# Rotary tables in two steps with a buffer of their own, squares in the projections' banks, rotation in two steps, expert scatters later

## What is computed

```python
xn = layernorm(x)
# attention: 16 query heads, 4 key/value heads, D = 128, an output gate
q, gate, k, v = split(xn @ w_qkv.T)
q = rope(layernorm(q, q_norm_w, q_norm_b))      # per head, with weight and bias
k = rope(layernorm(k, k_norm_w, k_norm_b))
attn = softmax(causal(q @ k.T / sqrt(D))) @ v
a = (attn * sigmoid(gate)) @ w_o.T
# experts: 8, the two best of each token
top, idx = top_k(xn @ w_router, 2); p = softmax(top)
f = sum_j p_j * (relu(xn @ w_fc[idx_j])**2 @ w_proj[idx_j])
return x + a + f
```

## Time and profile before

| what | value |
|---|---|
| runs, median (lowest to highest) | 1565.15 us (1564.32 to 1567.33), 3 runs |
| the profiled execution, its own time | 1559.9 us |
| its span | 1558.1 us |
| granted TensorE clock, mean | 0.998 of 2.4 GHz |

### The profile page before, as it was taken

How to read it: one execution, slowest core, us unless ns; L and a number is a source line. 1 busy time by engine, 2 the same in 40 slices (tenths; PEclk the granted TensorE clock), 3 DMA queues, 4 the chain that set the end, 5 groups by cost and what they waited for, 6 DMA issues and landing times.

```text
span 1558.1 us, 29980 instructions
## 1 busy us (share of the span) xinstructions
PE 1508.6 (97%) x10589; PEld 1379.8 (89%) x10589; DVE 1323.2 (85%) x3139; ACT 1154.4 (74%) x3013; POOL 522.8 (34%) x726
## 2 busy tenths in 40 slices
PE   4999999999899999999999999999999999999998
PEld 3788999999899999999888898999988888999997
DVE  7999888787899888787789988887778989988875
ACT  3777777777778777777778777777777777766775
POOL 5544434320453231221045332221014545343200
PEclk9999999999999999999999999999999999999999
DMA  4300010011111011101211100111001101102000
GB/s 143 138 5 20 22 42 21 20 32 50 45 34 30 27 34 30 32 27 34 71 45 33 32 25 11 46 30 32 28 30 62 33 5 39 32 20 62 20 8 8
DMA packets 46647, 56.66 MB, mean 36 GB/s; under 512 B 4576, under 2 KB 43232, under 8 KB 46304
## 3 DMA queue, kind: packets, MB, share of 16 engines
q1 hardware_dynamic: 43424, 46.34, 9.6%
q0 software_dynamic: 3072, 8.39, 1.7%
HBM read 42.40 MB, written 18.35 MB: 39 GB/s over the span
## 4 chain that ended last, share of the span: by engine, by line
PE 70%; DVE 23%; ACT 3%; issue 2%; POOL 1%; DMA 1%; SPq 0%; DVEq 0%; ACTq 0%; POOLq 0%
PE bank L1284 37%; PE o_bank L1284 18%; PE pt_bank L1359 12%; DVE pT_lo L1215 4%; DVE t_same L1170 3%; DVE neg_chunk_max L1201 3%; DVE bank L1198 2%; DVE t_same L1166 2%; DVE sumsq L1138 1%; ACT probs L921 1%; PE bank L1337 1%; DVE t_same L1154 1%; PE bank L1380 1%; DVE ogT_lo L1236 1%; DVE oT L1232 1%
## 5 line engine op out<-in xcount | busy, mean ns | idle before, releaser
L921 ACT ACTIVATE probs<-bank,neg_max 128x512 f32<-128x512 f32 (+3 forms) x640 | 399.2, 633 | 91.1 <-DVE neg_max L1208 80.1
L1215 DVE TENSOR_TENSOR pT_lo<-pt_bank,pT_hi 128x512 fp32r<-128x512 f32 (+1 forms) x576 | 368.1, 653 | 97.3 <-ACT pT_hi L940 94.8
L940 ACT ACTIVATE pT_hi<-pt_bank 128x512 fp32r<-128x512 f32 (+1 forms) x576 | 325.4, 578 | 128.6 <-PE pt_bank L1359 79.8
L1284 PE MATMUL o_bank<-pT_hi,v_hi 128*128 128x256 f32 x1088 | 333.8, 307 | 3.2 <-DVE pT_lo L1215 2.2
L786 POOL TENSOR_TENSOR t_swap<-qk_raw,table_swap 128x256 f32<-128x256 f32 (+1 forms) x256 | 135.9, 562 | 561.2 <-ACT t_same L890 560.2
L1359 PE MATMUL pt_bank<-ident_f,probs 128*128 128x128 f32 x2176 | 315.3, 273 | 9.2 <-DVE pT_lo L1215 8.7
L1284 PE MATMUL o_bank<-pT_hi,v_lo 128*128 128x256 f32 x1088 | 307.2, 282 | 0.0
L1284 PE MATMUL o_bank<-pT_lo,v_hi 128*128 128x256 f32 x1088 | 306.5, 282 | 0.0
L1201 DVE TENSOR_REDUCE neg_chunk_max<-bank 128x1 f32<-128x512 f32 (+1 forms) x384 | 244.7, 649 | 46.5 <-PE bank L1284 45.2
L1359 PEld LDWEIGHTS pt_bank<-ident_f,probs 128*128 128x128 f32 x2176 | 252.3, 140 | 35.0 <-DVE pT_lo L1215 12.5
L1284 PE MATMUL bank<-kT_hi,qT_hi 128*128 128x512 f32 (+3 forms) x640 | 243.7, 381 | 4.0 <-ACT probs L921 3.6
(11 more groups left out here) (163 smaller groups left out, 2967.7 us busy)
## 6 DMA issues: line engine op xcount, KB each, us to landing
rows<-xs SPq DMA_DIRECT2D x23, 256.0 KB, 2.6
expert_raw<-in_w_fc SPq DMA_DIRECT2D x23, 256.0 KB, 3.0
expert_raw<-in_w_proj SPq DMA_DIRECT2D x23, 256.0 KB, 2.7
yb<-rows SPq DMA_DIRECT2D x23, 256.0 KB, 2.1
xs<-in_x SPq DMA_DIRECT2D x11, 512.0 KB, 4.7
w_raw<-in_w_in SPq DMA_DIRECT2D x7, 640.0 KB, 4.0
angles<-in_cos_sin SPq DMA_DIRECT2D x64, 64.0 KB, 1.9
acc<-in_x SPq DMA_DIRECT2D x4, 512.0 KB, 8.2
```

Source lines behind the costliest of these rows:

```text
L921: act.activation(probs[:, u, h % 2, first:first + width], bank("scores", g, t, h, c)[:, 0:width], ACT.Exp, bias=neg_max[:, u, h % 2:h % 2 ...
L940: act.activation(pT_hi[:, n % PT_RING, 0:width], pt_bank[n % 2][:, 0:width], ACT.Copy)\
L1215: dve.tensor_tensor(pT_lo[:, n % PT_RING, 0:width], pt_bank[n % 2][:, 0:width], pT_hi[:, n % PT_RING, 0:width].bitcast(F32), ALU.subtract) ...
L1284: ins = pe.matmul(out_ap, s, m, start=(start and done == 1), stop=(stop and done == last))
```

## The change

It touches the rotation, the bank of Q, the scatters and the plan:
- `tables` keeps its first two instructions and no longer waits for the last rotation; a new step `bias_table` does the other three, waits for that rotation, and signals `bias_done`. `bias_part` has a buffer of its own. Loads that follow the tables on SP (angles, fills) wait for `bias_done`. `swap` waits for `both_done` of the tile before.
- ScalarE writes the squares in place, over Q and K in their banks. VectorE sums q's in `sumsq`, which now frees the bank of Q, and k's in `variance`, which waits for the v copy too. `q_take` no longer waits for KT; `same` does.
- `rope_b` is split in `rope_add` and `rope_b`, which also waits for the bias.
- Scatters begin at turn 44. All of `BEGIN` and `DUE` is new.

```diff
-SCATTER_AT, SCATTER_EVERY = 20, 3
+SCATTER_AT, SCATTER_EVERY = 44, 3
...
-FREED_BY = {"Q": "q_take", "KV": "v_lo", "G": "tanh", "QT": "q_lo", "KT": "k_lo", "GT": "og", "OUT": "out_add",
+FREED_BY = {"Q": "sumsq", "KV": "v_lo", "G": "tanh", "QT": "q_lo", "KT": "k_lo", "GT": "og", "OUT": "out_add",
...
-DUE = {"qkv": -43.81, "rope": -12.53, "turn": -314.72, "v_lo": -91.35, "gate": 7.24, "inv": -214.95,
-       "turn_gate": 4.73, "og": 4.02, "out": 10.53, "out_add": 1.16, "scores": -12.47, "max": -5.95,
-       "exp": 18.26, "prob_step": 1.95, "pv": 7.99, "p_hi": -283.79, "p_lo": -1.72, "moe": 348.73,
-       "moe_step": 36.0, "moe_evict": -19.57, "route": 89.48, "x1": 11.16, "x2": 38.95, "x3": 39.51,
-       "logits": -17.39, "gate_w": -102.68, "scatter": 143.34, "next_w": -59.05, "wo": 575.69, "comb": 73.3,
+DUE = {"tables": 119.68, "qkv": -43.65, "rope": -12.86, "turn": -330.08, "v_lo": -320.98, "gate": 6.81,
+       "inv": -159.64, "turn_gate": 0.47, "og": 3.56, "out": 16.07, "out_add": -3.77, "scores": -16.47,
+       "max": -9.82, "exp": 25.59, "prob_step": 1.96, "pv": 7.96, "p_hi": -411.68, "p_lo": -2.05, "moe": 342.11,
+       "moe_step": 36.02, "moe_evict": -113.96, "route": 128.28, "x1": 36.41, "x2": -411.08, "x3": 70.94,
+       "logits": -7.38, "gate_w": -220.11, "scatter": -82.13, "next_w": -60.45, "wo": 422.35, "comb": 461.7,
...
-            add("pool rope", ("tables", g, t), 4.0, [old(t1, "rope_b"), old(t1, "same"), ("angle_load", g, t),
-                                                     ("ln_tables",)], b0 + DUE["rope"])
+            add("pool tables", ("tables", g, t), 1.65, [old(t1, "swap"), old(t1, "same"), ("angle_load", g, t),
+                                                        ("ln_tables",)], b0 + DUE["tables"])
+            add("pool tables", ("bias_table", g, t), 2.4, [old(t1, "rope_b")], b0 + DUE["tables"])
...
-            add("dve rope", ("sumsq", g, t), 1.0, [("kv_take", g, t)], b0 + DUE["rope"])
-            add("dve rope", ("same", g, t), 0.93, [("kv_take", g, t), ("tables", g, t), old(t1, "rope_b")],
+            add("dve sumsq", ("sumsq", g, t), 0.68, [("q_take", g, t)], b0 + DUE["rope"])
+            add("dve sumsq", ("variance", g, t), 0.45, [("kv_take", g, t), old(t1, "rstd")], b0 + DUE["rope"])
+            add("dve rope", ("same", g, t), 0.93, [("kv_take", g, t), ("tables", g, t), old(t1, "KT")],
...
-            add("dve rope", ("rope_b", g, t), 2.2, [("swap", g, t), ("rstd", g, t)], b0 + DUE["rope"])
+            add("dve rope", ("rope_add", g, t), 0.8, [("swap", g, t), ("same", g, t)], b0 + DUE["rope"])
+            add("dve rope", ("rope_b", g, t), 1.5, [("rstd", g, t), ("bias_table", g, t)], b0 + DUE["rope"])
...
-        bias_part = t_swap[:, 0:2, :]
+        bias_part = sb("bias_part", [P, 2, D])
...
                     w.wait_ge(same_done, n)
                     w.wait_ge(swap_done, n)
+                    pool.tensor_tensor(halves(table_same[:]), halves(ln_w[:]), cos_t, ALU.mult)
+                    pool.tensor_tensor(halves(table_swap[:]), halves(ln_ws[:]), sin_t, ALU.mult).then_inc(tables_done, 1)
+                elif kind == "bias_table":
...
                     w.wait_ge(rotated_done, n)
-                    pool.tensor_tensor(halves(table_same[:]), halves(ln_w[:]), cos_t, ALU.mult)
-                    pool.tensor_tensor(halves(table_swap[:]), halves(ln_ws[:]), sin_t, ALU.mult)
                     pool.tensor_tensor(halves(table_bias[:]), halves(ln_b[:]), cos_t, ALU.mult)
-                    pool.tensor_tensor(halves(bias_part), halves(ln_bs[:]), sin_t, ALU.mult).then_inc(bias_parts, 1)
+                    pool.tensor_tensor(halves(bias_part[:]), halves(ln_bs[:]), sin_t, ALU.mult).then_inc(bias_parts, 1)
                     w.wait_ge(bias_parts, n + 1)
-                    pool.tensor_tensor(table_bias[:], table_bias[:], bias_part, ALU.add).then_inc(tables_done, 1)
+                    pool.tensor_tensor(table_bias[:], table_bias[:], bias_part[:], ALU.add).then_inc(bias_done, 1)
...
-                    if n:
-                        w.wait_ge(filled, fill["KT", *tile_before(g, t)])
                     act.activation(qk_raw[:, 0:HG, :], bank("Q", g, t)[:], ACT.Copy)
-                    act.activation(squares[:, 0:HG, :], bank("Q", g, t)[:], ACT.Square).then_inc(qkv_read, 1)
+                    act.activation(bank("Q", g, t)[:], bank("Q", g, t)[:], ACT.Square).then_inc(qkv_read, 1)
...
-                    act.activation(squares[:, HG, :], bank("KV", g, t)[:, 0:D], ACT.Square).then_inc(qkv_read, 1)
+                    act.activation(bank("KV", g, t)[:, 0:D], bank("KV", g, t)[:, 0:D], ACT.Square).then_inc(qkv_read, 1)
...
                 elif kind == "sumsq":
+                    w.wait_ge(qkv_read, 3 * (g * T + t) + 1)
+                    dve.tensor_reduce(sumsq[:, 0:HG], bank("Q", g, t)[:].rearrange("p (h d) -> p h d", d=D), AX.X, ALU.add)\
+                        .then_inc(sumsq_done, 1)
+                elif kind == "variance":
...
-                    w.wait_ge(qkv_read, 3 * n + 2)
-                    dve.tensor_reduce(sumsq[:], squares[:], AX.X, ALU.add).then_inc(sumsq_done, 1)
+                    w.wait_ge(qkv_read, 3 * n + 3)
+                    dve.tensor_reduce(sumsq[:, HG:HG + 1], bank("KV", g, t)[:, 0:D], AX.X, ALU.add).then_inc(k_sum_done, 1)
```

More of the change, by code:

```diff
@@ L198, in program_steps @@
     for k in range(FILLS):
-        add("sp fill", ("fill", k), 0.45, [("tables", 0, 1 + k // 3)], 30 + k, 512)
+        add("sp fill", ("fill", k), 0.45, [("bias_table", 0, 1 + k // 3)], 30 + k, 512)
     for t in range(T):
@@ L230, in program_steps @@
             if n_t >= 2:
-                add("sp angles", ("angle_load", g, t), 0.45, [old(t2, "tables")], b0 + DUE["rope"] - 15, 64)
-            add("pool rope", ("tables", g, t), 4.0, [old(t1, "rope_b"), old(t1, "same"), ("angle_load", g, t),
-                                                     ("ln_tables",)], b0 + DUE["rope"])
+                add("sp angles", ("angle_load", g, t), 0.45, [old(t2, "bias_table")], b0 + DUE["rope"] - 15, 64)
+            add("pool tables", ("tables", g, t), 1.65, [old(t1, "swap"), old(t1, "same"), ("angle_load", g, t),
+                                                        ("ln_tables",)], b0 + DUE["tables"])
+            add("pool tables", ("bias_table", g, t), 2.4, [old(t1, "rope_b")], b0 + DUE["tables"])
             add("pe QKV", ("Q", g, t), 1.39 if n_t else 2.6, [old(t1, "KT"), ("wq_lo", g, 1), ("xT_lo", 2 * (t // 4) + 1)],
@@ L238, in program_steps @@
                 b1 + DUE["gate"])
-            add("act QKV", ("q_take", g, t), 0.95, [("Q", g, t)] + [old(t1, x) for x in ("same", "swap", "KT")],
+            add("act QKV", ("q_take", g, t), 0.95, [("Q", g, t)] + [old(t1, x) for x in ("same", "swap")],
                 b0 + DUE["rope"])
@@ L243, in program_steps @@
                 b0 + DUE["rope"])
-            add("dve rope", ("sumsq", g, t), 1.0, [("kv_take", g, t)], b0 + DUE["rope"])
-            add("dve rope", ("same", g, t), 0.93, [("kv_take", g, t), ("tables", g, t), old(t1, "rope_b")],
+            add("dve sumsq", ("sumsq", g, t), 0.68, [("q_take", g, t)], b0 + DUE["rope"])
+            add("dve sumsq", ("variance", g, t), 0.45, [("kv_take", g, t), old(t1, "rstd")], b0 + DUE["rope"])
+            add("dve rope", ("same", g, t), 0.93, [("kv_take", g, t), ("tables", g, t), old(t1, "KT")],
                 b0 + DUE["rope"])
-            add("dve v", ("v_lo", g, t), 0.2, [("kv_take", g, t)], b0 + DUE["v_lo"])
-            add("pool rope", ("swap", g, t), 2.0, [("kv_take", g, t), old(t1, "rope_b")], b0 + DUE["rope"])
-            add("pool rope", ("rstd", g, t), 1.2, [("sumsq", g, t)], b0 + DUE["rope"])
-            add("dve rope", ("rope_b", g, t), 2.2, [("swap", g, t), ("rstd", g, t)], b0 + DUE["rope"])
+            add("dve v", ("v_lo", g, t), 0.2, [("variance", g, t)], b0 + DUE["v_lo"])
+            add("pool rope", ("swap", g, t), 2.0, [("kv_take", g, t), ("tables", g, t), old(t1, "rope_add")], b0 + DUE["rope"])
+            add("pool rope", ("rstd", g, t), 1.2, [("variance", g, t), old(t1, "rope_b")], b0 + DUE["rope"])
+            add("dve rope", ("rope_add", g, t), 0.8, [("swap", g, t), ("same", g, t)], b0 + DUE["rope"])
+            add("dve rope", ("rope_b", g, t), 1.5, [("rstd", g, t), ("bias_table", g, t)], b0 + DUE["rope"])
             last = len(chunks_of(t1[1])) - 1 if t1 else 0
@@ L483, in build @@
         t_same = sb("t_same", [P, HG + 1, D])
-        squares = rotated = t_same
+        rotated = t_same
         t_swap = sb("t_swap", [P, HG + 1, D])
@@ L609, in build @@
         freed_by = {
-            "Q": lambda g, t: (qkv_read, 3 * (g * T + t) + 1),
+            "Q": lambda g, t: (sumsq_done, g * T + t + 1),
             "KV": lambda g, t: (v_lo_done, g * T + t + 1),
@@ L659, in _ @@
                     first = 2 * SLOT * a[0]
-                    w.wait_ge(tables_done, 2 + a[0] // 3)
+                    w.wait_ge(bias_done, 2 + a[0] // 3)
```

(13 more changed lines are left out.)

11 lines of the change are left out of this document (9 added, 2 removed), and 20 rows, old and new, of the table BEGIN.

## The result

The changed kernel takes 1580.11 us (median of four runs, 1579.33 to 1580.79); beside it, four runs of the kernel before gave 1565.86. The ratio is 1.0089, with an interval of 1.0074 to 1.0103: 14.2 us slower, where 1558.2 was forecast and 1571 was the upper end of the range. The profiled execution took 1580.37 us, its span 1578.6. Its granted TensorE clock is 0.997 in mean, 0.998 before: a thousandth of the span, some 1.7 us at most.

A forecast was written before the change was run, and what follows sets the result against it. TensorE was taken to bound the kernel on average, VectorE and the tile chain where causal rows are short. Routing -6, loop -6, reductions +2, contention +2, bank +1 made -7 us: 1558.2 from 1565.15, range 1546 to 1571.

The forecast's parts named there:

- Contention: GpSimd tables running beside VectorE's add and rotation: 0.24 us a tile longer over 24 tiles; +2 us, bounds 0 and 12.5.
- Reductions: One VectorE reduction of squares becomes two: +0.17 us a tile, hidden in TensorE-bound stretches; +2 us, bounds 0 and 11.
- The loop: Chain from rotation to next rotation, about 11.4 us, at three later group starts: earlier tables gain 6 us, bounds 0 and 10.6.
- Routing: Routing's VectorE work, due 128.3 instead of 89.5, mostly leaves the full stretch before 140 us: -6 us, bounds 0 and 10.0.
- The bank: Q's bank is held until VectorE has reduced it, 0.683 us and a queue place longer: +1 us, bounds 0 and 22.
- the square into the bank: ScalarE's square written to the bank instead of SBUF: 0.598 against 0.596 us, so no cost.
- the late expert jobs: Later scatters push about two expert jobs from the TensorE-bound stretch to the one at 400 us: no cost.
- B: Rival: slower by contention in the 24 tiles where VectorE is full, 0.52 us a tile; +6.6, 1572; chance 0.21.
- A: Rival: the loop was hidden anyway, and VectorE's extra 10.0 us eats routing's gain; 1565; chance 0.21 with C and E.
- C: Rival: Q's longer bank hold stops TensorE in a third of 32 long tiles, costing 7; 1564; chance 0.21 with A and E.
- D: Rival: more than half of TensorE's idle is taken in both kinds of stretch, 16 us; 1549; chance 0.16.
- E: Rival: the plan still issues early table steps behind the rotation, losing the loop's 6; 1564; chance 0.21 with A and C.

## Why the prediction was wrong

Against the sum of -7 us, part by part; 14.2 is what has to come out.

**Contention (+2 taken, 0 to 12.5 as bounds; measured +12.7 to +15.5).** This is the step that failed. It was mis-sized three times over. The growth per tile was taken from the average of line 1236, an instruction that meets GpSimd by chance; the table step begins in 56 of 63 tiles as soon as the q product or rstd is done, and these two also free the add and the five steps of the rotation. The 1.20 us beside a table instruction was the nearer row. Second, it was charged in 24 tiles. By the starts and lengths of the single instructions, add and rotation grew by 12.1 us in the first eight tiles of the four groups (0.38 a tile, 0.24 taken) and by 5.9 in the last eight, against the kernel with the tables behind the rotation. Third, TensorE was said to feel a part. It felt 10.5 of the 12.1 in the short tiles and 3.3 of the 5.9 in the long ones (progress at the same turns of the profiled executions, start included). In the early tables of the kernel before the figures are 22.8 us lost for 17.6 grown in the short tiles, and 14.0 for 13.8 in the long ones; these executions lie 36.8 us apart and the medians 29.6, so some 7 us of it are not the edit's. So the regimes are there, but the long tiles are not cover: a longer rotation costs time in long tiles too, though VectorE has 41 of 260 us to spare from 140 to 400. Presumably the spare time lies in other places of its fixed queue; no run shows that.

**Reductions (+2 taken, 0 to 11; measured +6.5, and +6.6 in the kernel before).** The durations were right (+0.158 us a tile by the rows, 0.17 said). The variance step (0.248 to 0.320 us) was not in the sum. The second reduction cost 6.5 us of its 18, which is all of the 5.8 by which it lengthened VectorE's busy time; it was written off in 40 of 64 tiles by the same argument from VectorE's share. (The first reduction, 512 columns in place of 640, gives 8 of those 18 back; how much of that is felt is in the remainder below.)

**The loop (-6; measured 0 in the kernel before, at most 2.9 in the change).** Opening it in the kernel before, without the reads, gained nothing (1.0004), though there the two products still wait for all five table instructions; in the change the open loop with write-only tables is 2.9 us ahead of the closed one, of which VectorE's 2.5 us of busy time may be all. The prediction asked what is late next and named the right chain, the copy, the sum and the rotation, but then took half of the idle time for the tables because the waits for line 1170 were the longest. A wait names who came last, not why that one was late: GpSimd's swap waited for k's copy (575.8 us in 59 waits) and not for tables.

**Routing (-6; it hardly moved).** VectorE's routing instructions between 140 and 180 us take 2.64 us in all, of 9.8; the rest still runs before 140, though the due time went from 89.5 to 128.3. The prediction had named this as a sign of being wrong. The plan gives an idle engine what is ready, whatever its due time. What the move is worth stays open: the run with the old due time reached group 1 2.6 us later, with its whole order changed.

**The bank (+1; waits for sumsq 1.2 us in two)** was right, and so was "nothing" for the square into the bank and for the late expert jobs, as far as waits show: TensorE's waits for the expert jobs' features grew from 0.3 us to 1.6.

**What is left.** +12.7 (contention, by the tables behind the rotation) and +6.5 (second reduction) make 19.2, where 14.2 were lost. So the rest of the change (squares in the banks with the shorter first reduction, the split rotation, the late stores, the new order) gains about 5 us, in spite of what the two products of `same` and the variance step add to VectorE. The version with both losses removed says the same: 4.9 us under before. Which of these parts gains it is open; the two runs meant to part them could not.

**The rivals.** B was the case that came, by its mechanism and sign. It was to decide past 0.42 us more a tile; add and rotation grew by 0.28 a tile (18.0 us over 64, against the kernel with the tables behind the rotation) and the reductions by 0.16, together 0.44. Its place, 24 tiles, was too narrow, and its offset of 10 us for routing did not exist. A's "the loop was hidden anyway" was true, or nearly, as well. C, D and E did not occur: TensorE waits 1.2 us for the bank of Q, its idle time did not fall, and in 57 of 63 tiles the table steps begin between rstd's begin and the rotation.

## What to carry to other kernels

Before GpSimd work that reads SBUF is moved earlier, ask what event releases it, and which VectorE instruction the same event releases: two that one event frees meet in most rounds, and a chance average is no price for that. Ask the same where a wait is taken away: it may have kept two such instructions apart. An engine that is 85% busy with a fixed order gave hardly any cover here: charge what lengthens its busy time in full until a run says otherwise. And idle time in front of an instruction is worth removing only if what comes after does not wait for something else: follow the next wait before putting a gain to it.

## What the runs showed of the hardware

- A 128x128 scale-and-add on VectorE takes 0.343 us alone and 0.686 on average mostly beside a GpSimd product that reads SBUF, up to 0.829; in the kernel before with early tables 50 of them averaged 0.775, the longest 1.625. GpSimd pays too: its first table product averages 0.738 us in the kernel before and 0.915 with early tables. Beside GpSimd memsets neither step of VectorE grows (0.345 for the scale-and-add, 0.814 for the 640-wide add).
- The size of GpSimd's read counts: with the tables behind the rotation, 15 of the 64 adds lie mostly inside a GpSimd instruction, 12 in its 5-column rstd (1.3 us long in the mean) and three in the issue of a scatter or gather, and they average 0.814 us as the undisturbed ones do.
- Reading ScalarE's accumulator after the square of k took 0.200 us each time; VectorE's reduction of the same 128 columns from the bank took 0.283.
